# A megakernel's mixer: sixteen unrolled slots per row instead of a loop of twenty-four, with the next row prepared between the scans

## The reference

```python
x = x + mamba(layernorm(x))        # adds its own input once more
x = x + ternary_ffn(layernorm(x))  # a: up 128->512, gelu, down 512->128, RMS norms inside
x = x + gru(layernorm(x))          # b: minimal GRU, 512 wide, scan over the tokens
x = x + ternary_ffn(layernorm(x))  # c (d in the changed kernel): the same weights again

# mamba, 256 channels, 16 states
xi, z = split((layernorm(x) * gamma + beta) @ W_in)
u  = silu(conv4(xi) + b_conv)                 # causal, 4 taps, per channel
dt_r, B, C = split(u @ W_x)                   # x_dbl: 8, 16 and 16 columns
dt = softplus(dt_r @ W_dt + b_dt)
h[s] = exp(dt[s] * A) * h[s-1] + dt[s] * u[s] * B[s]     # 16 states n per channel
y[s] = sum_n h[s, n] * C[s, n] + u[s] * Dskip
out  = x + (y * silu(z)) @ W_out
```

## Time and profile before

| | us |
|---|---|
| median of 3 runs (1058.70 to 1060.96) | 1059.09 |
| profiled execution, own time | 1061.22 |
| its span, first to last instruction | 1059.4 |
| mean granted TensorE clock, of full speed | 0.852 |

### The profile page before, as it was taken

The page is one execution under the profiler, slowest core; times in us unless marked ns, Lnnn a source line. Parts: engine busy times, 40 slices in busy tenths (PEclk is TensorE's granted clock), DMA queues, the critical chain, the costliest instruction groups (busy, mean ns, idle before and its releaser), DMA issues. The chain is left out here.

```text
span 1059.4 us, 12336 instructions
## 1 busy us (share of the span) xinstructions
PE 771.0 (73%) x4122; PEld 628.3 (59%) x4122; DVE 801.9 (76%) x1094; ACT 560.8 (53%) x923; POOL 514.6 (49%) x337
## 2 busy tenths in 40 slices
PE   2445557668868698569966897769956997597884
PEld 1234445546766488447855687548845786376673
DVE  3799579868986899868996899779996899324231
ACT  2555465466635764467545764477446754441502
POOL 2287137533751487237742585238733485224321
PEclk9688856878888899689978899789977997899896
DMA  5100000000000000000000000000000000000000
GB/s 131 48 1 0 11 0 1 1 10 1 1 1 1 11 1 11 1 10 0 10 0 10 0 0 10 0 10 0 10 0 0 1 4 9 0 1 11 1 11 10
DMA packets 16901, 8.86 MB, mean 8 GB/s; under 512 B 5328, under 2 KB 15328, under 8 KB 16864
## 3 DMA queue, kind: packets, MB, share of 16 engines
q1 hardware_dynamic: 16864, 8.39, 2.9%
HBM read 6.29 MB, written 2.10 MB: 8 GB/s over the span
## 5 line engine op out<-in xcount | busy, mean ns | idle before, releaser
L832 DVE TENSOR_TENSOR_SCAN state<-dA,inflow 128x1024 f32<-128x1024 f32 x128 | 292.0, 2281 | 31.0 <-ACT dA L569 30.4
L409 POOL TENSOR_TENSOR inflow<-dtu,b_all 128x1024 f32<-128x1024 f32 x112 | 274.5, 2451 | 75.0 <-ACT b_all L559 73.5
L568 ACT ACTIVATE dA<-dt,decay_c 128x512 f32<-128x512 f32 x128 | 88.4, 690 | 214.7 <-DVE state L832 209.4
L838 DVE TENSOR_TENSOR state<-state,c_ps 128x1024 f32<-128x1024 f32 x128 | 153.3, 1198 | 7.2 <-PE c_ps L1111 6.9
L1118 PE MATMUL y_ps<-ident,state 128*128 128x128 f32 x1024 | 158.1, 306 | 0.5 <-DVE state L838 0.5
L1118 PEld LDWEIGHTS y_ps<-ident,state 128*128 128x128 f32 x1024 | 141.8, 160 | 15.5 <-issue 5.8
L1111 PE MATMUL c_ps<-xd,pick 128*128 128x512 f32 x128 | 71.4, 558 | 97.6 <-DVE state L838 93.6
L1026 PE MATMUL work<-in_hi,wzh_hi 128*128 128x512 f32 x256 | 102.3, 399 | 1.7 <-ACT wide L628 1.4
L1111 PEld LDWEIGHTS c_ps<-xd,pick 128*128 128x128 f32 x128 | 27.7, 216 | 126.1 <-DVE state L838 117.6
L1027 PE MATMUL work<-in_hi,wzh_lo 128*128 128x512 f32 x256 | 101.1, 395 | 0.0
L1028 PE MATMUL work<-in_lo,wzh_hi 128*128 128x512 f32 x256 | 100.9, 394 | 0.0
(11 more groups left out here) (169 smaller groups left out, 1702.2 us busy)
## 6 DMA issues: line engine op xcount, KB each, us to landing
x_tok<-in_x SPq DMA_DIRECT2D x8, 256.0 KB, 2.8
out_x<-x_tok SPq DMA_DIRECT2D x8, 256.0 KB, 2.3
wide<-in_Wz SPq DMA_DIRECT2D x1, 1024.0 KB, 11.3
wide<-in_Wh SPq DMA_DIRECT2D x1, 1024.0 KB, 13.4
skip_f<-in_W SPq DMA_DIRECT2D x2, 256.0 KB, 3.8
dtu<-in_W_in SPq DMA_DIRECT2D x1, 256.0 KB
x_tok<-in_w_up SPq DMA_DIRECT2D x1, 256.0 KB, 2.9
x_tok<-in_w_down SPq DMA_DIRECT2D x1, 256.0 KB, 3.1
```

The costliest lines, as they stand in the source:

```text
L409: pool.tensor_tensor(inflow[:, n % 2, :, :], dtu[:, :, :], b_all[:, n % 2, :].unsqueeze(1).broadcast_to([P, HALVES, SEQ]), ALU.mult).then_ ...
L568: act.activation(dA[:, 0, :], dt[:, 0, :], ACT.Exp, scale=decay_c[:, 0, n:n + 1])
L832: dve.tensor_tensor_scan(flat(state[:, n % 3, :, :]), flat(dA[:, :, :]), flat(inflow[:, n % 2, :, :]), 0.0, ALU.mult, ALU.add).then_inc(s_ ...
L838: dve.tensor_tensor(state[:, n % 3, :, :], state[:, n % 3, :, :], c_ps[:, :].unsqueeze(1).broadcast_to([P, HALVES, SEQ]), ALU.mult).then_i ...
```

## The change

The loop is unrolled, a row has 16 slots, one per state, and a piece of work stands at a number of slots after (or before) its row's first scan: `due(r, s, at)` gives the row b = r - at // 16 whose piece falls into slot s of row r. The scans have 0 to 15, the next row's preparation -22 to -2, layer a 18 to 26, the GRU 26 to 37, the second FFN (now d) 38 to 44. The rest:

- The projection goes to the work banks, of which there are three (b_ps is gone), each with a fixed order of products; TensorE waits for the bank's last reader.
- Convolution: ScalarE makes the four tap products from PSUM, GpSimd adds three to the first, 1024 columns at a time.
- Silu of u and z: one 1024-column instruction each, together, in slot 10.
- The relu of softplus and the sum for dt are one VectorE instruction for each half, from PSUM; b_dt comes through a row of ones in the product.
- The skip product is a matmul with a diagonal of Dskip. VectorE makes one remainder of xd instead of two.
- B: x_dbl's sixteen rows are copied to SBUF, stored to DRAM, and loaded again, each row into all partitions, with four buffers. GpSimd makes all sixteen inflows.
- x, base, z, xd and dt have two buffers. Tail weights are issued after row 0's B has been stored and its first four loads issued.

```diff
-SCAN = 4
-BACK = SCAN + STATE
-SLOTS = BACK + 4
-LAG = {"a": 1, "b": 2, "c": 3}
+FIRST, LAST = -2, ROWS + 2
+BANKS = 3
+def due(r, s, at):
+    b = r - at // STATE
+    return [b] if at % STATE == s and 0 <= b < ROWS else []
...
+            def b_store(b):
+                sp.wait_ge(s_brow, b + 1)
+                sp.dma_start(b_dram[b % 2, :, :], b_row[B_AT:B_AT + STATE, :]).then_inc(s_bstored, 16)
+                sp.wait_ge(s_bstored, 16 * b + 16)
+            def b_load(b, n):
+                wait(sp, s_inflow, STATE * b + n - RING + 1)
+                sp.dma_start(b_all[:, n % RING, :], b_dram[b % 2, n, :].partition_broadcast(P)
+                             ).then_inc(s_bring[n % RING], 16)
...
+            load_x(1)
+            b_store(0)
+            for n in range(RING):
+                b_load(0, n)
...
+            def mix_conv(b, s):          # GpSimd
+                if s == 1:
+                    evacuated(pool, b, "xi0")
+                    evacuated(pool, b, "xi1")
+                else:
+                    pool.wait_ge(s_conv, (TAPS - 1) * b + s - 1)
+                pool.tensor_tensor(u[:, :, s:SEQ], u[:, :, s:SEQ], tapped[s - 1][:, :, 0:SEQ - s], ALU.add
+                                   ).then_inc(s_conv, 1)
...
+                for b in due(r, s, s):   # GpSimd, slot s
+                    if s + 2 < STATE:
+                        mix_inflow(b, s + 2)
...
+                for t in due(r, s, 43):
+                    ffn_rms(t, "d")
+                for b in due(r, s, -21):
+                    mix_root(b)
+                for t in due(r, s, 27):
+                    for j in range(FB):
+                        gru_in_lo(t, j)
...
+                act.activation(u[:, h, :], bank(p)[:, :], ACT.Identity, bias=b_conv_c[:, h:h + 1],
+                               scale=taps_c[:, h, TAPS - 1:TAPS])
+                for s in range(1, TAPS):
+                    last = act.activation(tapped[s - 1][:, h, :], bank(p)[:, :], ACT.Identity,
+                                          scale=taps_c[:, h, TAPS - 1 - s:TAPS - s])
...
+                for b in due(r, s, -6):  # ScalarE, slot 10
+                    act.preload_act_table(ACT.Silu)
+                    mix_silu_u(b)
+                    mix_silu_z(b)
+                for t in due(r, s, 26):
+                    for j in range(2 * FB):
+                        gru_in(t, j)
+                for b in due(r, s, -6):
+                    act.preload_act_table_set("natural_log_exp_and_others")
+                for b in due(r, s, -5):
+                    mix_xd(b)
+                for b in due(r, s, -4):
+                    mix_softplus(b)
+                for t in due(r, s, 28):
+                    gru_gate(t, 0)
...
+                for b in due(r, s, s):   # VectorE, slot s
+                    mix_scan(b, s)
+                for t in due(r, s, 16):
+                    mix_gate(t)
+                for b in due(r, s, s):
+                    mix_read(b, s)
...
+                for t in due(r, s, 16):  # TensorE
+                    mix_gt(t, 0)
+                    mix_gt(t, 1)
+                for b in due(r, s, 0):
+                    mix_skip(b)
+                    mix_cn(b, 0)
...
+                for t in due(r, s, 36):
+                    gru_out(t)
...
+                for t in due(r, s, 25):
+                    norm_t(t, 2)
+                for t in due(r, s, 41):
+                    ffn_down(t, "d")
+                for t in due(r, s, 26):
+                    for j in range(2 * FB):
+                        gru_in(t, j)
...
+                for b in due(r, s, -5):
+                    mix_xdbl(b)
+                for t in due(r, s, 43):
+                    ffn_sumsq(t, "d")
+                for t in due(r, s, 27):
+                    gru_gate(t, "z0")
+                for b in due(r, s, -4):
+                    mix_dtp(b, 0)
+                    mix_dtp(b, 1)
+                for t in due(r, s, 29):
+                    gru_gate(t, "h0")
+                    gru_gate(t, "z1")
...
+                for b in due(r, s, s):
+                    if s + 1 < STATE:
+                        mix_cn(b, s + 1)
+                    mix_acc(b, s)
```

## The result

The changed kernel takes 1142.52 us (median of 4 runs, 1139.51 to 1146.28), the kernel before 1059.05. The ratio is 1.079, 95% interval 1.075 to 1.082: 7.9% slower, where 994 us and 6% faster were forecast. The range (930 to 1045) missed it; even rival C, the one that ended on the slower side, gave only 1117.

What follows compares the result with a forecast made beforehand. VectorE was taken as bound during the scans, no engine in the 36.5 us gap. Floor 81.6 plus waits 31 gave 112.5 us a row; start 44, rows 78, 92.5, 562.5, 102 and end 115 gave 994 us, range 930 to 1045.

Steps and rivals of the forecast that it cites:

- rival C: Not faster: TensorE falls to its lower clock while waiting in the queue; row of 130, total 1117 us; chance 0.11.
- Waits that the one list makes: Per-slot delays to VectorE from in-order lists, with C's broadcast last on TensorE: 29.9 us a row, rounded up to 31.
- the 5.0 of lengthened instructions: Slots 2, 6 and 9: four-column factor instructions meeting a long GpSimd instruction, 1.2 + 2.3 + 1.5 = 5.0 us.
- 32 matmuls, some 3.7 us: Slot 5: length taken for the GRU's output, which comes before C 5 and makes a 3.2 us wait.
- A's sum: Likeliest case, waits as placed: row 107 to 118 us, total 994 us, by itself 955 to 1033; chance 0.55.
- The sign that the prediction gave for C: A granted TensorE clock under 0.8 would show that the low-clock case, not the forecast, holds.
- The floor's 7.6 us for four gates: VectorE's four gates with their 512-column scans, 7.6 us of the 28.6 us a row beside scans and reads.
- hand-made floor: VectorE's work by sums alone: 53.0 us of scans and reads plus 28.6 of other work, 81.6 us a row.
- The rule of the Trainium skill cited against the change: GpSimd and second-port VectorE instructions block each other, so moved adds aren't free; without such meetings the row would be 107.5.
- Rival B: VectorE is the bound, most waits overlap as late reads let others catch up: row 100 gives 907 us, 105 gives 941; chance 0.25.
- Rival D: Loads of B or the weights behind them come late, in row 0 or at the start: 1010 to 1020 us; chance 0.09.
- the 8 allowed: Row 0: 8 us added for weights arriving late behind B's store and first loads, within row 0's 78 us.

Runs made afterwards that it cites:

- Run 6: Changed kernel with half the terms of both FFNs' down products and the GRU's output left out (result not the reference's): 1097.18 us.
- run 4: Changed kernel plus 32 identity transposes a row on TensorE as filler before the gated row's transposes in slot 0: 1123.81 us.
- run 9: run 7 with the next scan ahead of other work in slots 1, 5, 7, 10 and 11, plus 40 filler transposes a row in slot 9: 1025.08 us.
- run 5: Changed kernel with the convolution back on VectorE, ScalarE's taps and GpSimd's adds gone: 1182.77 us.
- run 7: Changed kernel with C ahead of long products in slots 0, 4, 9, 11, 13, C 1 before skip products, in_lo before two roots: 1052.66 us.

## Why the prediction was wrong, step by step

**The places were right.** A wait for C stands behind each product that the prediction named, and in the full rows it missed none of over 0.6 us. Of VectorE's other waits it missed one, 1.3 us in slot 8 for the mean square of layer a.

**The step that failed is the size of "Waits that the one list makes"**: 24.9 us a row of idle VectorE were priced (29.9 less the 5.0 of lengthened instructions), 40.6 are measured, and the 86.6 of its work came out at 92.6. In parts:

| wait for C | forecast | measured | ahead of C in after's records |
|---|---|---|---|
| slot 0 | 3.1 | 5.9 | transposes 1.97 and skip 3.62 |
| slot 5 | 3.2 | 6.5 | GRU output 4.38 + 3.74 |
| slot 10 | 3.1 | 6.3 | norm 2 1.12, down product 5.49 |
| slot 12 | 5.1 | 5.8 | z0, twelve matmuls, 5.1 |
| slot 14 | 1.7 | 3.6 | h0 and z1, 24 matmuls, 7.2 (5.6 forecast) |

- *The count.* "32 matmuls, some 3.7 us" took plain float32 products at the duration of a transpose. They are recorded twice each. Run 6 gives the price for the down products and the GRU's output: 6.9 us a row, 45 in all. The eight skip products were taken at 1.03 us in the same way and are 1.95 at the full clock (run 4), 0.9 us more in slot 0 that run 6 doesn't cover. It was a misread of the trace before, not a thing it hid.
- *The clock.* The prediction had this as rival C, all or nothing: 18 us a row with a chance of 0.11. A third of it is simply what happens: the granted clock is 0.68 to 0.93 in the four slots shown. At the full clock the skip, transposes, down product and z0 would be 1.95, 1.09, 3.74 and 2.9 us instead of 3.62, 1.97, 5.49 and 5.1: an estimate of 6.5 us a row, which overlaps in part with the 6.9 above. Runs 4 and 9 show it for two of the places, 18.7 and 12.1 us. It should have been a term of A's sum: TensorE is idle 4.6 us before slot 0's transposes, 6.0 before norm 2's and 4.3 before z0, and all of them ran slow. The sign that the prediction gave for C, a granted clock under 0.8, is an average that doesn't show this: it was 0.81 over the run, and 0.85 in row 4.
- *VectorE's own 6 us.* Four-column instructions met by GpSimd cost 5.5 us a row by the groups (`den`, `offset`, `rden`, over 0.16 us for an undisturbed one), near the 5.0 forecast. The GRU's scans average 1.86 us where an undisturbed one takes 1.22: 2.6 us a row. The floor's 7.6 us for four gates (0.75 + 1.15 each) has room for the short ones alone. A read directly behind its scan starts 2.32 us after it, where the read of the kernel before started 2.20 after the scan ahead of it: 16 times 0.12 is 1.9. The remaining 1 us is the hand-made floor, not resolved further.

The rule of the Trainium skill cited against the change (SBUF — State Buffer, section "SBUF: two separate sides") named a cost that is there. For the adds that the change moved it is small: run 5 puts their share at 1 us a row.

**Rival B** was far off: late reads didn't let the others catch up, since the list has the next C wait for the read before it (`mix_cn` waits on `s_read`). **Rival D**: the 128 loads of B land in 3.2 us and no instruction waits for them; W_h and W_z hold scan 2 of row 0 for 5.4 us, within the 8 allowed. The start was 0.9 us under the forecast, row 0 6.2 over, row 1 17.2, row 7 11.4 and the tail 13.2. In the tail TensorE's clock is 0.82 (0.88 before), and the same mis-counted products stand there; that these make the excess was not tested by a run of its own.

**So why slower than before?** The change removed the 36.5 us gap, and put all of its work and the products of three chains between reads, on a TensorE list with C at each slot's end. Order alone (run 7) takes back 90 us and gives the kernel before minus 0.6%; with five scans moved ahead as well, and filler before one product, it is 3.2% faster. What stays open: what it would take to bring the full row of run 7 well under its 116.0, of which VectorE is busy 93.7. Its largest direct waits in rows 2 to 6 are for the GRU's output (5.2 us a row), in_hi (4.2), C (3.9) and the mean square of d (2.1).

## What to carry to other kernels

When a broadcast that the bottleneck engine needs every few microseconds shares an in-order list with bulk products, put it ahead of them in every slot; in one slot alone, most of the wait moved to the next. Price a product by its own row in the trace (records times mean), not by the nearest instruction of its shape, and where TensorE waits ahead of a product, price the product at the low clock as well: a mean clock of the run doesn't tell. Moving an engine's critical instruction forward delays what stands behind it, and the engine that waits for that may be the one you wait for.

## What the runs showed of the hardware

- Plain float32 128x128 products leave two records per issued matmul, 0.117 us each at the full clock (3.74 / 32); identity transposes leave one.
- Idle TensorE time can have a price after it. Work that computes nothing shortened the kernel by 18.7 us in one place and 12.1 in another. The Trainium skill, TensorE: Matmul & The Clock Gate, section "Part 1: The HAM clock gate", gives two levels in the ratio of two, 1.2 and 2.4 GHz; the skip products' 3.62 against 1.95 us, a ratio of 1.86, is near it.
- The slow stretch need not start with the first matmul after the pause. In slot 14 of row 4 TensorE is idle 3.76 us before h0, whose first four matmuls are recorded at 0.4 to 0.5 us, the following at 0.63, and z1's again at 0.4.
- The clock isn't local. With filler in slot 9 (run 9) the skip products of slot 0 took 3.0 to 3.6 us in rows 3 to 6, where without it they took 1.95 in each: what one filler gives can be lost elsewhere. Single slots of single rows are no measure; medians of the whole are.
